# One attention head at a time on TensorE: score tiles interleaved with P times V and the side products

## The reference

```
qkv = (x @ Wqkv.T + bqkv).reshape(B, S, 3, H, HD).transpose(2, 0, 3, 1, 4)
attn = softmax(einsum('bhid,bhjd->bhij', q, k) / sqrt(HD))
coh = sigmoid(tanh(comb @ Wc1.T + bc1) @ Wc2.T + bc2).transpose(0, 2, 1)
mod = attn * coh[..., None];  mod = mod / (mod.sum(-1, keepdims=True) + 1e-08)
mod = (1.0 - fi) * mod + fi * fa[:, None, :, None]
out = einsum('bhij,bhjd->bhid', mod, v) ... @ Wout.T + bout
x = x + out
# then: gate, softmax, top 2 of 8 experts, three layers per expert, weighted sum, residual
```

## Time and profile before

| what | value |
|---|---|
| median of three runs | 1123.45 us |
| profiled execution, its own time | 1124.42 us |
| its span | 1122.4 us |
| attention's slots with scores | about 80 to 604 us |
| TensorE busy | 972.4 us (87%) |
| VectorE busy | 746.4 us (67%) |
| ScalarE busy | 549.1 us (49%) |
| mean granted TensorE clock | 0.917 |

### The profile page before, as it was taken

One profiled execution on the slowest core, in us unless ns is written; L12 is line 12 of the kernel. 1 busy time (PEld: TensorE's weight loads), 2 busy tenths in 40 slices (PEclk: granted clock), 3 DMA queues, 4 the chain that ended last, 5 costly groups with the idle time before them and its releaser, 6 DMA issues.

```text
span 1122.4 us, 24379 instructions
## 1 busy us (share of the span) xinstructions
PE 972.4 (87%) x7142; PEld 582.8 (52%) x7143; DVE 746.4 (67%) x1546; ACT 549.1 (49%) x1129; POOL 609.6 (54%) x738
## 2 busy tenths in 40 slices
PE   3789998898989889898878678989949999999993
PEld 1323333323323233232324567877838989898992
DVE  6478888786868868688874565555726656555562
ACT  2227786665857667575675344322313333333330
POOL 3324345355453445434136353767948787877874
PEclk9689999988989889899896888999969999999997
DMA  4716171513526043261254453454313232332322
GB/s 145 113 48 95 39 114 63 73 57 95 98 78 90 24 108 65 78 96 37 80 165 167 160 152 105 119 159 113 67 40 59 39 58 40 56 52 44 58 39 29
DMA packets 76527, 93.09 MB, mean 83 GB/s; under 512 B 18824, under 2 KB 69024, under 8 KB 74144
## 3 DMA queue, kind: packets, MB, share of 16 engines
q1 hardware_dynamic: 60048, 72.10, 26.9%
q0 software_dynamic: 14304, 19.15, 10.2%
q10 hardware_dynamic: 2096, 0.84, 0.3%
HBM read 60.21 MB, written 38.68 MB: 88 GB/s over the span
## 4 chain that ended last, share of the span: by engine, by line
PE 67%; DVE 10%; DMA 7%; issue 6%; ACT 5%; POOL 2%; SPq 1%; another core or an unknown queue 1%; ACTq 0%; DVEq 0%; POOLq 0%
PE bank L915 23%; PE bank L746 9%; PE bank L800 9%; PE bank L733 7%; PE bank L929 7%; ACT arena L1051 3%; PE bank L722 3%; DVE mx L1156 3%; DMA x_tile<-xs 3%; DMA out<-y,y_dest 2%; PE bank L806 2%; PE bank L874 2%; PE bank L889 2%; POOL out L615 1%; DVE arena L1420 1%
## 5 line engine op out<-in xcount | busy, mean ns | idle before, releaser
L1156 DVE TENSOR_REDUCE mx<-bank 128x1 f32<-128x512 f32 x512 | 327.2, 683 | 81.4 <-PE bank L722 56.5
L1051 ACT ACTIVATE arena<-bank 128x512 f32<-128x512 f32 x512 | 278.2, 597 | 87.7 <-PE bank L733 71.8
L608 POOL TENSOR_TENSOR hl<-hf,hh 128x256 f16<-128x256 f32 x316 | 237.8, 1121 | 128.5 <-DVE y_dest L1396 79.8
L1083 ACT ACTIVATE hf<-bank,w_b 128x256 f32<-128x256 f32 x316 | 132.5, 470 | 281.8 <-PE bank L915 277.9
L1379 DVE CAST hh<-hf 128x256 f16<-128x256 f32 x316 | 150.5, 497 | 132.4 <-ACT hf L1083 120.3
L915 PE MATMUL bank<-hh,arena 128*128 128x256 f16 x1248 | 215.7, 280 | 0.9 <-issue 0.9
L733 PE MATMUL bank<-arena 49*128 49x512 f16 x512 | 172.2, 404 | 28.6 <-issue 13.8
L722 PE MATMUL bank<-arena 48*128 48x512 f16 x512 | 173.9, 403 | 20.3 <-DVE mx L1156 20.2
L915 PE MATMUL bank<-hl,arena 128*128 128x256 f16 x624 | 174.2, 279 | 0.0
L746 PE MATMUL bank<-arena 128*17 128x512 f32 x1024 | 146.1, 644 | 0.3 <-issue 0.3
L915 PEld LDWEIGHTS bank<-hh,arena 128*128 x1248 | 125.1, 100 | 19.8 <-issue 2.5
(11 more groups left out here) (217 smaller groups left out, 1067.8 us busy)
## 6 DMA issues: line engine op xcount, KB each, us to landing
raw<-in_we SPq DMA_DIRECT2D x16, 1024.0 KB, 5.4
arena<-parts_dram SPq DMA_DIRECT2D x96, 128.0 KB, 7.1
x_tile<-xs SPq DMA_DIRECT2D x41, 256.0 KB
parts_dram<-arena SPq DMA_DIRECT2D x16, 512.0 KB
xs<-in_pads SPq DMA_DIRECT2D x8, 816.0 KB, 6.3
arena<-in_xT SPq DMA_DIRECT2D x8, 512.0 KB, 4.5
arena<-in_x SPq DMA_DIRECT2D x8, 512.0 KB, 6.0
out<-rows SPq DMA_DIRECT2D x8, 512.0 KB, 5.2
```

The lines of the kernel that those rows point to most:

```text
L608: nc.gpsimd.tensor_tensor(hl[which][:, par, m, :], hf[which][:, par, m, :], hh[which][:, par, m, :], ALU.subtract).then_inc(lo[which], 1)
L1051: nc.scalar.activation(pr[:, s % TT, n, :], b_bank[no % B_RING][:, :], ACT.Exp, scale=SCALE).then_inc(b_read, 1)
L1083: nc.scalar.activation(hf[which][:, par, m, :], layer[which][m // 2][:, m % 2 * TS:(m % 2 + 1) * TS], ACT.Relu, bias=bias[which][:, bass.d ...
L1156: V.tensor_reduce(mx[:, g % 2, s % TT, c:c + 1], a_bank[no % A_RING][:, :], X, ALU.max).then_inc(a_read, 1)
```

## The change

The four pairs of a slot are issued one head at a time, with something between each two of them. P times V of the slot before now follows the first pair instead of the second. The products of the slot, `mt` among them, are put in one list `here`; its first half (rounded down) stands between the second and the third pair, the rest between the third and the fourth. A slot with one product has nothing between its second and third pair.

```diff
         for s in range(FIRST, LAST):
-            scores(s, (0, 1))
+            here = shift_task(s) + tasks(s)
+            scores(s, (0,))
             if scored(s - 1):
                 pv(s - 1)
-            for t in shift_task(s):
+            scores(s, (1,))
+            for t in here[:len(here) // 2]:
                 product(t)
-            scores(s, (2, 3))
-            for t in tasks(s):
+            scores(s, (2,))
+            for t in here[len(here) // 2:]:
                 product(t)
+            scores(s, (3,))
```

## The result

The changed kernel took 1188.86 us in the median of four runs (1187.5 to 1193.25), against 1122.84 us (1119.23 to 1123.75) for the kernel before. The ratio is 1.0601, with a 95% interval of 1.0564 to 1.0639: 66 us slower. The forecast was 1175 us, in a range of 1148 to 1200. The profiled execution took 1189.97 us, with a span of 1188.0 us.

The account below looks back on a forecast made before the run. In quiet stretches TensorE's own instruction stream was taken as the bound. Batches 2 to 5 +23.2, batch 1 +6.9, batch 6 +9.1, batch 0 +8.8 and batch 7 +3 made +51.0 on 1124.4 us: 1175 us, range 1148 to 1200.

Parts of the forecast that it names:

- P times V would wait for the exponential of pair 3: Quiet slots: P times V waits 0.55 us for the previous slot's last exponential, bounds 0.45 and 0.75.
- A divided slot costs 0.10 us: Quiet slots with two or more products: a third group of score pairs adds 0.10 us, 0.8 us per batch.
- the quiet slots: Slots 2 to 10 and 13 to 15, forecast to take 6.9 us more per batch in all.
- `mt` waits for VectorE's split: Three slots of a batch: `mt` waits 0.25 us for the split maxima, 0.8 us per batch, bounds 0 and 2.
- Old stalls on exponentials go: Quiet slots: earlier waits on exponentials disappear, 0.9 us less per batch, bounds 0.5 and 1.4.
- Slots 11 and 12 give 2.2 us back in four batches: P times V fills TensorE's idle time before a tile held up by VectorE: -2.2 us each in batches 2 to 5.
- Batch 0, batch 7, the experts: Batch 0 takes 8.8 us more, batch 7 takes 3 us more, and the part behind the slots changes by 0.
- Two slots at the turn of a batch pay the new wait: Slots 15 to 1: the "remote" standstill stays as it is and two slots pay the wait, +1.1 us per batch.
- Rival (a): TensorE's new pauses drop the clock to 1.2 GHz in a third of the quiet slots: 1281 us, chance 0.08.
- if granted clock in the quiet slots leaves 1.00: One of the prediction's signs of being wrong: the granted clock in slots 2 to 10 and 13 to 15 departs from 1.00.
- Rival (b): Filled stalls keep the clock up; faster if the new wait is below 0.37 us a slot: 1103 us, chance 0.06.
- Rival (c): VectorE or "remote" waits pace half of the slots, where the new wait costs nothing: 1149 us, chance 0.18.

Follow-up runs that it names:

- e6: The changed kernel with the exponential of head 3 done over 256 of 512 queries, the rest of that P left stale: 1167.3 us, ratio 1.0415.
- e7: The kernel before with the last exponential of a slot done over 256 of 512 queries, the rest stale: 1119.4 us, ratio 0.9981.
- e2: The changed kernel with pair 3 moved in front of the second half of the products, next to pair 2: 1141.1 us, ratio 1.0167.
- e1: The changed kernel with P times V put back behind the second pair, products still divided: 1189.5 us, ratio 1.0616.
- e3: The changed kernel with the products undivided, all between pairs 2 and 3: 1181.3 us, ratio 1.0526.
- e5: The kernel before with the order of e2 in slots 0, 1 and 12 only: 1121.8 us, ratio 1.0021.

## Why the prediction was right

- *P times V would wait for the exponential of pair 3, with 1.07 us from tile to P.* Right: 1.08 us in the timeline of the changed kernel, and an idle time of 0.47 us before P times V in almost every quiet slot (0.53 forecast); P times V then takes 1.05 in the chain in place of 0.98. Over the kernel it is 53.1 us in 106 waits, the longest of them, up to 4.1, in slots 0. Shown by e6 and e7, which shorten just this exponential; in slot 9 of e2 the wait is gone. Incomplete in one point: e1 showed that the bank of B tile 3 holds the loop at the same length even if P times V stands later.
- *A divided slot costs 0.10 us.* Too small: 0.21 to 0.24 in slots 3, 7 and 9 (e3). I counted the added group of pairs and not the product that now starts behind one. Over slots 2 to 10 of six batches e3 gave back 6.2 us, where the sum has 4.2 for them: 2 of the 7.2 us by which the quiet slots came out above the forecast.
- *`mt` waits for VectorE's split, 0.8 us per batch.* Wrong: in no quiet slot of batches 1 to 6 did `mt` wait. Such a late wait came in slot 2, where another product's transpose (L806) stood idle 0.30 us for GpSimd's sum. In the trace that sum waits for VectorE's `take`, and the `take` for A tile 3, now the last thing of slot 1. That is 0.3 us per batch, on the transpose and not on `mt`. No run tried this chain by itself; in e1 and e3 slot 2 stayed at 4.67 us (3.55 before).
- *Old stalls on exponentials go, 0.9 us per batch.* Right in part. Slot 5, 0.4 us above its stream before, now runs without a stall. Slots 4 and 8 grew by 0.46 and 0.45 us, little less than the new wait, and in slot 4 B tile 3 still waits 0.43 us behind ScalarE's other work. How much went in all, no run shows.
- *Slots 11 and 12 give 2.2 us back in four batches.* The filled idle time was right, what it gives too large: -5.4 us in place of -8.8. P times V did fill the idle time, and slot 11 fell from 5.6 to 3.2 us, while slot 12, where the wait for VectorE now stands, grew from 5.6 to 7.2. I left out the next wait on the same routing steps, the counts', 8.8 us in seven waits. The clock then fell in slot 13 of batches 4 and 5, which took 6.2 us for 3.95; beside the other batches (4.69) that is 3.0 us, counted among the quiet slots, and nothing in the prediction had it.
- *Batch 0, batch 7, the experts.* Within 2 us each.
- *Two slots at the turn of a batch pay the new wait, 1.1 us.* The sum is right (+7.7 in seven turns), and that is luck in good part: the seven turns changed by -1.1 to +2.6 us, and P times V waited there up to 4.1 us, not 0.5. Why ScalarE and VectorE stand still together at the turn stays open; slots 0 and 1 together took 10.1 us in e2 and 12.8 in e5 with the same order in both.
- *Rival (a), the clock.* Out as a cause of the 66 us: the clock was 1.00 in 69 of the 72 quiet slots of batches 1 to 6, with TensorE busy for 88% of the nine slots shown. The other three are slot 13 of batches 4, 5 and 6, behind the waits of slot 12, and by the prediction's own sign ("if granted clock in the quiet slots leaves 1.00") that much of it was wrong. *Rival (b), not slower*: out, the wait was 0.50 us on average against a limit of 0.37. *Rival (c), half of the slots cover it*: out, 106 of 128 slots show the wait.

So the main term held and was tested. That 1189 lies only 14 us from 1175 is owed in part to small terms that were off in both directions: dividing and the clock of slot 13 cost more, `mt` less, slots 11 and 12 gave less.

## What to carry to other kernels

Before work is moved between a producer and its consumer, add up what lies between them along the issuing engine and compare it with the round trip (here 1.07 us from a tile's start to its P: 0.42 to the reader, 0.60 for it, 0.05 back). Spreading four tiles evenly looked better balanced, but put the last tile of a slot next to the first thing that needs it; the cover that counts is that of the tightest pair, over the slot's border too. And look for every user of the same release: taking P times V away left the bank's next tile waiting for it.

## What was not expected of the hardware

The same six matmuls took 0.69 us in the chain behind a transpose and 0.80 behind a pair of score tiles; the first pair behind other work took 0.32 and a second pair 0.22. The Trainium skill, "TensorEngine Tiling (Array Packing)", section "Key Properties", says that a change of the tiling mode drains the array. The trace agrees in kind and shows a price on both sides of a group, 0.21 us or a little more per added group in slots 3, 7 and 9 of e3; that it is the drain which costs this, no run shows.

The routing step that holds up slots 11 and 12 is itself stretched: its instruction of 32 elements per row took 2.27 us from 376.76, while a GpSimd instruction of 1024 per row ran from 376.63 to 378.98, and one of the same form at 382.58, with no such neighbour, took 0.19. No run moved the two apart.
